# First row group's mean and variance by VectorE's statistics instruction, and weight loads of 112 partitions with the last rows apart

## Time and profile before

| | |
|---|---|
| device time, three runs | 590.26, 590.72, 590.88 us; median 590.72 |
| the profiled execution's own time | 591.18 us |
| its span in the trace | 589.1 us (granted clock 1.0) |
| PE busy | 580.1 us, 98% of the span |
| PEld busy | 539.7 us, 92% |
| DVE busy | 512.3 us, 87% |
| POOL busy | 456.2 us, 77% |
| ACT busy | 357.1 us, 61% |
| DMA moved | 30.67 MB, mean 52 GB/s |

### The profile page before, as it was taken

How to read it: one execution, slowest core, us unless ns; L and a number is a source line. 1 busy time by engine, 2 the same in 40 slices (tenths; PEclk the granted TensorE clock), 3 DMA queues, 4 the chain that set the end, 5 groups by cost and what they waited for, 6 DMA issues and landing times. The chain is left out here.

```text
span 589.1 us, 16421 instructions
## 1 busy us (share of the span) xinstructions
PE 580.1 (98%) x6750; PEld 539.7 (92%) x6750; DVE 512.3 (87%) x1232; ACT 357.1 (61%) x497; POOL 456.2 (77%) x361
## 2 busy tenths in 40 slices
PE   7999999999999999999999999999999999999997
PEld 7999998899989998899989998899989998999997
DVE  4887979889998999979998999979998999978764
ACT  5778895555586555765576545764576545544441
POOL 3417569999689977999689977999679977997930
PEclk9999999999999999999999999999999999999999
DMA  9710220002210103001220113002220101002021
GB/s 207 169 73 1 72 73 2 2 2 73 81 63 2 73 23 124 2 2 72 74 73 1 47 36 137 2 1 74 72 73 2 47 27 60 16 2 73 1 73 74
DMA packets 10395, 30.67 MB, mean 52 GB/s; under 512 B 944, under 2 KB 4048, under 8 KB 10320
## 3 DMA queue, kind: packets, MB, share of 16 engines
q1 hardware_dynamic: 10320, 29.62, 16.0%
HBM read 21.23 MB, written 8.39 MB: 50 GB/s over the span
## 5 line engine op out<-in xcount | busy, mean ns | idle before, releaser
L502 PE MATMUL acc<-wd,hop 114*128 114x128 f16 (+1 forms) x2944 | 170.9, 219 | 0.7 <-POOL hop L1417 0.6
L502 PEld LDWEIGHTS acc<-wd,hop 114*128 114x128 f16 (+1 forms) x2944 | 167.4, 98 | 1.9 <-POOL hop L1417 0.8
L734 ACT ACTIVATE pk<-acc 114x512 f32<-114x512 f32 (+1 forms) x120 | 70.7, 590 | 84.7 <-PE acc L390 50.7
L1402 POOL TENSOR_TENSOR hs<-hx 114x512 f32<-114x512 f32 x47 | 60.9, 1295 | 55.5 <-DVE hx L1142 52.2
L1417 POOL TENSOR_TENSOR hop<-hs,hop 114x1024 f16<-114x1024 f32 x46 | 98.2, 2136 | 3.9 <-ACT hop L789 3.9
L1414 POOL TENSOR_TENSOR hop<-hx,hop 114x1024 f16<-114x1024 f32 x45 | 96.2, 2137 | 1.3 <-ACT hop L778 1.3
L390 PE MATMUL acc<-xop,wu 128*128 128x256 f16 x704 | 84.2, 273 | 0.3
L390 PE MATMUL acc<-xop,wg 128*128 128x256 f16 x704 | 84.2, 273 | 0.2
L397 PE MATMUL acc<-xop,wu 128*128 128x256 f16 x704 | 84.2, 273 | 0.1
L397 PE MATMUL acc<-xop,wg 128*128 128x256 f16 x704 | 84.1, 273 | 0.2 <-DVE acc L1085 0.2
L1045 DVE TENSOR_TENSOR bd<-acc,pk 114x256 f32<-114x256 f32 (+1 forms) x104 | 43.6, 419 | 45.5 <-ACT pk L734 45.4
(11 more groups left out here) (172 smaller groups left out, 932.6 us busy)
## 6 DMA issues: line engine op xcount, KB each, us to landing
xr<-in_x SPq DMA_DIRECT2D x16, 512.0 KB, 4.3
zx<-in_x SPq DMA_DIRECT2D x16, 512.0 KB, 3.6
out_y<-zx SPq DMA_DIRECT2D x15, 512.0 KB, 2.6
hop<-in_w_down SPq DMA_DIRECT2D x1, 1364.0 KB, 19.7
hop<-in_w_gate SPq DMA_DIRECT2D x2, 576.0 KB, 9.6
hop<-in_w_up SPq DMA_DIRECT2D x1, 1152.0 KB
out_y<-zx SPq DMA_DIRECT2D x2, 256.0 KB, 2.3
hop<-in_w_gate SPq DMA_DIRECT2D x1, 192.0 KB
```

Source lines behind the costliest of these rows:

```text
L502: last = nc.tensor.matmul(acc[:, bank[n], s // 2, at:at + P], operand(g, c, t, form, level), wd[0:WIDE[c], slot, c, :], start=which == 0 a ...
L734: nc.scalar.activation(pk[0:rows, q % 2, :, :], pair[:, :, T:2 * T], ACT.Copy, scale=XS if u[0] == "X" else 1.0).then_inc(copied, 1)
L1402: nc.gpsimd.tensor_tensor(hs[:, 4:8:2, :], h[:, 0:4:2, :], h[:, 1:4:2, :], ALU.add)
```

## The change

Statistics: DVE now makes mean and variance of both tiles of the first group with the statistics instructions: two `bn_stats` of 512 columns for each tile, and one `bn_aggr`, into a part of the buffer `bd`; then one small multiply makes minus the means. ACT's four steps before `normalise(0, 0)` go. POOL's `rstd(0)` starts from the variance, and signals `ln_done` ahead of `onep`, which has a semaphore of its own.

Loads: gate and up are loaded with partitions 0 to 111 in place of 0 to 95 and 96 to 111 apart. Gate's partitions 112 and 113 are issued by ACT; up's by SP behind the down weights. SP no longer has a gate DMA of small size, and `w_in[0]` and `w_in[1]` are complete at 48. PE's idle work goes from 62, 4 and 12 transposes to 46, 8 and 14.

```diff
@@ buffers @@
+        stats = bd[:, 0, 0, 0:12 * NT].rearrange("p (t i) -> p t i", t=NT)
+        mv = bd[:, 1, 0, 0:2 * NT].rearrange("p (t i) -> p t i", t=NT)
@@ SP @@
             sp.wait_ge(row_zero, 1)
-            for lo, hi in ((96, 112), (112, 113)):
-                sp.dma_start(stage[0][lo:hi, :].rearrange("p (j e) -> p j e", j=NJ),
-                             w_gate[:, NC * lo:NC * hi, :].rearrange("j (p c) d -> p j (c d)", c=NC)).then_inc(w_in[0], 16)
-            sp.dma_start(stage[0][113:114, :].rearrange("p (j e) -> p j e", j=NJ)[:, :, 0:2 * DB],
-                         w_gate[:, NC * 113:HB, :].rearrange("j (p c) d -> p j (c d)", c=2)).then_inc(w_in[0], 16)
             for j, signal in ((0, w_in[0]), (NJ // 2, gate_rest)):
-                sp.dma_start(stage[0][0:96, :].rearrange("p (j e) -> p j e", j=NJ)[:, j:j + NJ // 2, :],
-                             w_gate[j:j + NJ // 2, 0:NC * 96, :].rearrange("j (p c) d -> p j (c d)", c=NC)).then_inc(signal, 16)
+                sp.dma_start(stage[0][0:112, :].rearrange("p (j e) -> p j e", j=NJ)[:, j:j + NJ // 2, :],
+                             w_gate[j:j + NJ // 2, 0:NC * 112, :].rearrange("j (p c) d -> p j (c d)", c=NC)).then_inc(signal, 16)
             sp.wait_ge(row_zero, 2)
-            for lo, hi in ((0, 96), (96, 112), (112, 113)):
-                sp.dma_start(stage[1][lo:hi, :].rearrange("p (j e) -> p j e", j=NJ),
-                             w_up[:, NC * lo:NC * hi, :].rearrange("j (p c) d -> p j (c d)", c=NC)).then_inc(w_in[1], 16)
+            sp.dma_start(stage[1][0:112, :].rearrange("p (j e) -> p j e", j=NJ),
+                         w_up[:, 0:NC * 112, :].rearrange("j (p c) d -> p j (c d)", c=NC)).then_inc(w_in[1], 16)
+            sp.dma_start(down_stage, w_down.rearrange("j o h -> o j h")).then_inc(w_in[2], 16)
+            sp.dma_start(stage[1][112:113, :].rearrange("p (j e) -> p j e", j=NJ),
+                         w_up[:, NC * 112:NC * 113, :].rearrange("j (p c) d -> p j (c d)", c=NC)).then_inc(w_in[1], 16)
             sp.dma_start(stage[1][113:114, :].rearrange("p (j e) -> p j e", j=NJ)[:, :, 0:2 * DB],
                          w_up[:, NC * 113:HB, :].rearrange("j (p c) d -> p j (c d)", c=2)).then_inc(w_in[1], 16)
-            sp.dma_start(down_stage, w_down.rearrange("j o h -> o j h")).then_inc(w_in[2], 16)
@@ PE @@
-                        pe.wait_ge(w_in[m], 64 if m < 2 else 16)
+                        pe.wait_ge(w_in[m], 48 if m < 2 else 16)
-            idle_work(62)
+            idle_work(46)
             weights(("T", 0, 0), range(0, 4))
-            idle_work(4)
+            idle_work(8)
             weights(("T", 0, 0), range(4, NJ))
             x_unit(("X", 0, 0))
             total(0, ("T", 0, 0))
             x_unit(("X", 0, 1))
-            idle_work(12)
+            idle_work(14)
@@ ACT @@
+            act.wait_ge(row_zero, 1)
+            act.dma_start(stage[0][112:113, :].rearrange("p (j e) -> p j e", j=NJ),
+                          w_gate[:, NC * 112:NC * 113, :].rearrange("j (p c) d -> p j (c d)", c=NC)).then_inc(w_in[0], 16)
+            act.dma_start(stage[0][113:114, :].rearrange("p (j e) -> p j e", j=NJ)[:, :, 0:2 * DB],
+                          w_gate[:, NC * 113:HB, :].rearrange("j (p c) d -> p j (c d)", c=2)).then_inc(w_in[0], 16)
-                act.wait_ge(w_in[m], 64 if m < 2 else 16)
+                act.wait_ge(w_in[m], 48 if m < 2 else 16)
-            act.wait_ge(x_in[0], 16)
-            nc.scalar.activation(junk[:, :], xr[:, 0, :], ACT.Copy, accum_out=sm[:, 0:1]).then_inc(sum_done, 1)
-            act.wait_ge(sum_done, 1)
-            nc.scalar.activation(nm[:, 0:1], sm[:, 0:1], ACT.Copy, scale=-1.0 / D).then_inc(first_mean, 1)
-            row_var(0, 0)
-            row_var(0, 1)
             normalise(0, 0)
...
+                    act.wait_ge(onep_done, g + 1)
                     nc.scalar.activation(zx[:, t, :], zx[:, t, :], ACT.Identity, bias=nmrs[:, k:k + 1], scale=onep[:, k:k + 1]).then_inc(z_done, 1)
@@ DVE @@
-            dve.wait_ge(x_in[1], 16)
-            nc.vector.tensor_reduce(sm[:, 1:2], xr[:, 1, :], AX.X, ALU.add).then_inc(second_sum, 1)
-            dve.wait_ge(second_sum, 1)
-            nc.vector.tensor_scalar_mul(nm[:, 1:2], sm[:, 1:2], -1.0 / D).then_inc(second_mean, 1)
-            dve.wait_ge(w_in[0], 64)
+            for t in range(NT):
+                dve.wait_ge(x_in[t], 16)
+                for i in range(2):
+                    nc.vector.bn_stats(stats[:, t, 6 * i:6 * i + 6], xr[:, t, D // 2 * i:D // 2 * (i + 1)]).then_inc(stats_done, 1)
+                dve.wait_ge(stats_done, 2 * t + 2)
+                nc.vector.bn_aggr(mv[:, t, :], stats[:, t, :]).then_inc(var_done, 1)
+            dve.wait_ge(var_done, NT)
+            nc.vector.tensor_scalar_mul(nm[:, 0:NT], mv[:, :, 0], -1.0).then_inc(sum_done, 1)
+            dve.wait_ge(sum_done, 1)
+            dve.wait_ge(w_in[0], 48)
@@ POOL, rstd(g) @@
-                nc.gpsimd.tensor_scalar(vr[:, two], vr[:, two], 1.0 / D, EPS, ALU.mult, ALU.add).then_inc(newton, 1)
+                if g == 0:
+
+                    nc.gpsimd.tensor_scalar(vr[:, two], mv[:, :, 1], 1.0, EPS, ALU.mult, ALU.add).then_inc(newton, 1)
+                else:
+                    nc.gpsimd.tensor_scalar(vr[:, two], vr[:, two], 1.0 / D, EPS, ALU.mult, ALU.add).then_inc(newton, 1)
...
-                nc.gpsimd.tensor_tensor(nmrs[:, two], nm[:, two], rs[:, two], ALU.mult)
-                nc.gpsimd.tensor_scalar_add(onep[:, two], rs[:, two], 1.0).then_inc(ln_done, 1)
+                if g == 0:
+                    pool.wait_ge(sum_done, 1)
+                nc.gpsimd.tensor_tensor(nmrs[:, two], nm[:, two], rs[:, two], ALU.mult).then_inc(ln_done, 1)
+
+                nc.gpsimd.tensor_scalar_add(onep[:, two], rs[:, two], 1.0).then_inc(onep_done, 1)
```

More of the change, by code:

```diff
@@ L257, in octonion_ffn_attention_kernel @@
         hpair_done = sem("hpair_done"); hs_done = sem("hs_done"); hhs_done = sem("hhs_done"); h_ready = sem("h_ready")
-        sum_done = sem("sum_done"); mean_done = sem("mean_done"); first_mean = sem("first_mean"); second_sum = sem("second_sum"); second_mean = sem("second_mean"); var_done = sem("var_done");
-        newton = sem("newton"); ln_done = sem("ln_done"); norm_done = sem("norm_done"); dot_done = sem("dot_done")
+        sum_done = sem("sum_done"); mean_done = sem("mean_done"); stats_done = sem("stats_done"); var_done = sem("var_done");
+        newton = sem("newton"); ln_done = sem("ln_done"); onep_done = sem("onep_done"); norm_done = sem("norm_done"); dot_done = sem("dot_done")
         power_done = sem("power_done"); bound_done = sem("bound_done"); z_done = sem("z_done"); tail_mult = sem("tail_mult"); tail_high = sem("tail_high"); tail_odd = sem("tail_odd"); tail_pair = sem("tail_pair"); tail_sum = sem("tail_sum"); tail_ready = sem("tail_ready"); out_done = sem("out_done")
@@ L642, in row_var @@
                 k = NT * g + t
[L643 to L649, removed]
+                act.wait_ge(mean_done, g)
+                act.wait_ge(sum_done, NT * g + 1)
+                act.wait_ge(var_done, k)
                 nc.scalar.activation(dump(g), xr[:, t, :], ACT.Square, bias=nm[:, k:k + 1], accum_out=vr[:, k:k + 1]).then_inc(var_done, 1)
```

## The result

The changed kernel takes 592.57 us (median of 9 runs, 592.15 to 593.40) against 591.18 for the kernel before in the same runs: ratio 1.0027, 95% interval 1.0018 to 1.0035. It is 1.4 us slower. The forecast was 1.5 us faster: 589.2 us, with a range of 588.3 to 591.2.

What follows compares the result with a forecast made beforehand. PE's own work was taken to bound everything after the first product. The sum was -1.5 us at the start, 0 for up and 0 for the rest, taking the median from 590.72 to 589.2 us, range 588.3 to 591.2.

Steps and rivals of the forecast that it cites:

- PE bounds the rest, S is the gain: Whole kernel: if the first product, at 18.32 us, comes earlier by S, so does the end; S taken as 1.5 us.
- Statistics: Before the first product: POOL starts at 8.8 in place of 10.01, ACT's normalisation ends at 12.4 us, just in time.
- Gate's wide loads: Gate's load: without narrow loads' rate valleys, 1.4 us lost in each, the second half lands at 12.2 in place of 13.77.
- The single rows' issue: ACT's two DMAs for gate's single rows: some 0.44 us each to issue, in idle time, so no cost.
- The absolute-sums step: DVE before the first product: if w_in[0] comes by 9.9, sums and normalisation end by 13.4 us, on time.
- the floor: PE's own idle work ahead of gate's second half: ready at 12.20, so the gain is at most 1.57 us.
- Rival B: Gate lands little sooner (second half 12.95, 589.9 us) or the statistics instruction is slow (590.2 us); chance 0.14.
- Up's rows behind the down weights: Up's load: w_in[1] complete at 21.5 us; up to 22.0 no cost, beyond it every microsecond is one of PE.
- A: Up's last rows come late, w_in[1] between 22.0 and about 24.9; net -1.5 to +1.2, about 590.2 us; chance 0.18.
- C: Down weights delay up's last rows to 26.9; PE's up transposes at 31.95, 3.2 us slower, 593.9 us; chance 0.08.
- PE's idle work: PE before the first product: 16 fewer warm transposes at 0.11 us each, -1.74 us; 4 more in the middle, +0.44.
- The cost outside the span: Around the program: no term; profiled time 591.18 with span 589.1 was to become 589.7 with 587.6.

Runs made afterwards that it cites:

- e1: The changed kernel with gate's partitions 112 and 113 issued by SP ahead of the wide halves, no DMA by ACT: 590.23 us, ratio 0.9987.
- e7: The changed kernel with ACT issuing gate's two single rows at about 1.7 us, ahead of its table load: 590.29 us, ratio 0.9988.
- e16: e1 with gate's partitions 96 to 111 again a load of their own, ahead of the wide halves of 96: 591.53 us, ratio 1.0007.
- e12: The kernel before with the wide loads (gate's single rows by SP), old statistics and idle work of 44, 2 and 14: 589.50 us, ratio 0.9971.
- e2: The changed kernel with DVE normalising tile 1 ahead of its first sum of gate: 591.35 us, ratio 1.0009.
- e10: e1 with DVE sums and ACT sums of squares replacing the statistics instruction, and onep's own semaphore taken out: 590.17 us, ratio 0.9978.
- e17: The kernel before with wide loads (gate's rows by SP), idle work 46, 8, 14, old statistics, 16 empty instructions in DVE's list: 589.44 us.
- e14: The kernel before with wide loads (gate's rows by SP), idle work 46, 8, 14, old statistics, one semaphore less: 589.56 us, ratio 0.9973.
- e4: The kernel before with the new statistics alone, loads and idle work as before: 591.70 us, ratio 1.0011.

## Why the prediction was wrong

**PE bounds the rest, S is the gain.** Right. In the profiles of e1 and of the kernel before the first product differs by 16.43 - 18.32 = -1.89 and the span by -2.0. In all twenty profiles, from the first product at 15.76 (e7) to 18.60 (the changed kernel), the span less the start of the first product lies between 570.6 and 570.9 us.

**Statistics.** Right in direction, and better than costed: a pass of 512 takes about 0.65 (0.61 was taken), the combining step 0.21 (0.15), but tile 1 of x landed by 6.1 and not at 7.15, so POOL started at 7.82 where 8.8 was forecast.

**Gate's wide loads.** The mechanism, that narrow loads cost the valleys, is right for the 16 partitions (e16) and wrong for the single rows: in e1 they stand in the same queue and make none. Its size was underrated. The forecast of 12.2 for gate's second half was too late: it landed at about 11.5 in the changed kernel and at 11.12 in e12, where PE waited for it, against 13.92 in e16 with the 16 partitions apart. That is 2.8 us for the one load, where 1.4 was taken.

**The single rows' issue: the step that failed in the span.** The prediction put it as "It has nothing else to do before 11.2, so nothing", and took w_in[0] at 9.7. The issue indeed cost ACT nothing: it took 1.26 and 0.64 us in place of 0.44 each, in time in which ACT was idle. What was never costed was when such a load would be *served*: ACT issues it at 3.74 and 5.03, when SP's queue already holds gate, up and the down weights. Its packets ran at 9 to 11 us and w_in[0] was complete at 11.9. DVE's 1.75 us sum and, behind it, the normalisation moved by the same amount. The absolute-sums step had named that queue and its condition ("If w_in[0] comes by 9.9"), but no rival gave the case in which it fails by 2 us. e1, e7 and e2 show each link: with the rows served early the span is 587.4, 1.6 below the kernel before. That the forecast said 1.5 is in part luck: it let gate's landing at 12.2 decide, and in e1 that landing did not decide. PE went from its own idle work to gate and to the x transposes at 12.23 without a gap, so the gain is that of the floor, 1.57.

**Rival B** came nearest, "the two single rows still hold some DMA engines up, from another queue", but it was wrong in kind: they were held up themselves. The rule of the Trainium skill, DMA: Bandwidth & Descriptors, section "Issuing engines are not separate DMA queues", was cited there as a rule against that part, by which only time of issue can be saved; e1 and e7 agree with it. From ACT at 1.69 us or from SP the span is the same (587.5 and 587.4), so the other queue brought nothing. That the same loads issued 2 us later cost 2.2 us of span is beyond what it says.

**Up's rows behind the down weights, rivals A and C.** Both fell. w_in[1] was complete by 21.07, when ACT took up absolute(1) without any wait, against the limit of 22.0 and the forecast of 21.5; PE's up transposes at 29.02 had no idle time ahead of them. In e1 ACT did wait for it, until 20.85:

```profile
20.85 2.76 ACT L666 ACTIVATE hop<-hop 114x3072 f16<-114x3072 f32 x1 [1.91 <-DMA hop<-in_w_up]
```

**PE's idle work.** The price holds, but only as an average. Between the two profiles the 16 transposes taken away were worth 9.14 - 6.65 = 2.49 us and not 1.74. That is the chance of two executions: 46 of them took 6.41 to 7.91 us in the fourteen profiles that have them, 7.28 in the mean, and 62 took 8.60 to 9.51 in four, 9.02 in the mean. The difference of the means is 1.74. In e1 and the kernels like it, where PE waits for nothing else, the span follows that length:

```profile
3.52 6.41 PEld L431 LDWEIGHTS acc<-ident 128*128 128x128 f32 x46 [3.52 <-POOL ident L1348]
```

```profile
3.52 7.89 PEld L435 LDWEIGHTS acc<-ident 128*128 128x128 f32 x46 [3.52 <-POOL ident L1353]
```

The first is e7's, with a span of 586.4 us, the second e10's, with 587.9.

**The cost outside the span** had no term at all: the second step that failed. The prediction carried the 2.1 us around the program over unchanged (591.18 with a span of 589.1 to 589.7 with 587.6), without giving a reason. It was 2.8 for the changed kernel. Of the 2.9 us between the change that was forecast (-1.5) and the one measured (+1.4), about 2.2 lie in the span and 0.7 here. (The forecast of 589.2 is 3.4 below 592.57; the other 0.5 is that the kernel before, too, took more in the later runs, 591.18 against 590.72.) The loss in the span is explained and undone; of the one outside only that it comes with the statistics part is shown, and what in it makes it stays open.

## What to carry to other kernels

A load moved to an idle engine was free to issue here and not free to wait for: ask what is in the queues at the moment of its issue, and what stands on each engine behind the semaphore that it completes. If a small load gates a large one's semaphore, issue it first. Compare time less span between kernels as well as spans: a part of a change can cost there, and no row of an engine will say so. And take the price of a stretch like PE's idle work from several executions: one pair gave 2.49 us where the mean is 1.74.

## What the runs showed of the hardware that was not expected

- A load of 16 partitions (192 KB) pulls the DMA rate of all that runs beside it down to 108 to 156 GB/s for 3 us and delays the landing of a load issued ahead of it, from 6.0 us at the latest to 7.35 (e16 against e1). Loads of a single partition in the same queue did not.
- Two loads of 20 KB together, issued by ACT from 3.74 us on beside a loaded SP queue, were complete at 11.9 us; issued from 1.69 on, they were complete by 8.4 (the changed kernel and e7).
- The first idle transposes of PE run at about half the rate of the later ones, at a granted clock of 1.00 (full speed, 2.4 GHz) throughout, and the moment of the change differs by execution: 46 of them took between 6.41 us (e7) and 7.91 us (e17), with the same instructions. By stretches of one microsecond (length, PE's busy time, count, clock, DMA share, GB/s) the kernel before has six to a stretch until 8.5 us, then eleven:

```profile
7.50:8.50 1.00, 1.00 (x6) 1.00 1.03 154
8.50:9.50 1.00, 1.00 (x11) 1.00 1.10 249
```

  Where PE waits for nothing else this goes into the span (586.4 us with 6.41, 587.9 with 7.89). That it makes the scatter between runs of one kernel is likely and not shown, since each kernel has one profile.
- The time around the span is not a constant: its medians ran from 1.87 us (e14) to 2.98 us (e4, e16) for programs that do the same work.
